# A transformer decoder layer in fp32 on one core: ring order of the cross attention, and row halves for the retention scores

## The reference

```python
# retention, H = 16 heads of HD = 16 channels
ret  = einsum('bhid,bhjd->bhij', q, k) * D            # D: decay mask, causal
ret  = ret / clip(abs(ret.sum(-1)), 1, None)
g    = einsum('bhij,bhjd->bhid', ret, v)
g    = (g - g.mean(-1)) / sqrt(g.var(-1) + 1e-5)      # per head
x    = x + (silu(xn @ Wg + bg) * (g * gn_w + gn_b)) @ Wo + bo
# cross attention, 16 heads, 64 channels after the products of weights
scores = einsum('bhsr,bhlr->bhsl', q_r, k_r)          # 1600 x 1444 for each row of the batch
ctx_c  = softmax(scores) @ kv_r                       # 1444 x 64
x      = x + (ctx_c -> w_kc_kv -> Wo)
# feed-forward with ternary weights
x      = x + bitlinear(sigmoid(x1) * x2, w3)
```

## Time and profile before

| what | us |
|---|---|
| median of 3 runs | 2492.05 |
| the profiled execution's own time | 2489.71 |
| its span | 2487.9 |
| TensorE busy, of the span | 2297.7 (92%) |
| GpSimd busy | 1841.3 (74%) |
| VectorE busy | 1689.2 (68%) |
| ScalarE busy | 1189.3 (48%) |

### The profile page before, as it was taken

The page is one execution under the profiler, slowest core; times in us unless marked ns, Lnnn a source line. Parts: engine busy times, 40 slices in busy tenths (PEclk is TensorE's granted clock), DMA queues, the critical chain, the costliest instruction groups (busy, mean ns, idle before and its releaser), DMA issues. The chain is left out here.

```text
span 2487.9 us, 47277 instructions
## 1 busy us (share of the span) xinstructions
PE 2297.7 (92%) x15380; PEld 1443.5 (58%) x15380; DVE 1689.2 (68%) x2816; ACT 1189.3 (48%) x1925; POOL 1841.3 (74%) x827
## 2 busy tenths in 40 slices
PE   7899857999995999999999999999999999998398
PEld 4454536777772555555555555555555555554388
DVE  5888847888875666666666666666666666660575
ACT  3232312223222665665665665665666666663143
POOL 2444444998883799899899899899898998998111
PEclk9999978999996999999999999999999999999699
DMA  4000015666664424333333333333333343230111
GB/s 136 14 20 20 19 30 158 186 188 172 185 178 115 97 62 90 89 66 85 89 70 84 86 74 86 80 78 86 76 83 83 74 88 83 69 73 13 40 46 40
DMA packets 229954, 212.21 MB, mean 85 GB/s; under 512 B 115542, under 2 KB 204842, under 8 KB 229760
## 3 DMA queue, kind: packets, MB, share of 16 engines
q1 hardware_dynamic: 229888, 211.37, 34.4%
HBM read 128.17 MB, written 59.48 MB: 75 GB/s over the span
## 5 line engine op out<-in xcount | busy, mean ns | idle before, releaser
L1680 POOL TENSOR_TENSOR x_acc<-x_acc,x_prob 120x1600 f32<-120x1600 f32 (+1 forms) x320 | 1154.3, 3607 | 34.0 <-ACT x_prob L1701 11.1
L1701 ACT ACTIVATE x_prob<-x_scores 120x800 f32<-120x800 f32 (+1 forms) x768 | 601.8, 837 | 19.0 <-PE x_scores L1877 11.2
L1897 PE MATMUL x_context<-x_prob,x_kv 120*64 120x400 f32 (+1 forms) x3072 | 600.6, 512 | 0.0
L1796 DVE TENSOR_REDUCE x_mx<-x_ring 115x2 f32<-115x1024 f32 (+1 forms) x341 | 418.2, 1226 | 47.8 <-PE x_ring L1944 29.7
L1805 DVE TENSOR_REDUCE x_mx<-x_ring 115x1 f32<-115x420 f32 (+2 forms) x320 | 199.7, 624 | 225.3 <-PE x_ring L1951 225.3
L1897 PEld LDWEIGHTS x_context<-x_prob,x_kv 120*64 120x64 f32 (+1 forms) x3072 | 186.2, 136 | 261.3 <-issue 261.3
L1721 ACT COPY x_half<-x_ring 115x420 f32<-115x420 f32 (+2 forms) x320 | 171.6, 536 | 329.1 <-PE x_ring L1951 329.1
L1877 PE MATMUL x_scores<-x_qh,x_dh 64*120 64x400 f32 (+1 forms) x1536 | 274.0, 351 | 1.0 <-DMA x_dl<-x_dl 0.3
L1877 PE MATMUL x_scores<-x_ql,x_dh 64*120 64x400 f32 (+1 forms) x1536 | 267.1, 342 | 0.0
L1877 PE MATMUL x_scores<-x_qh,x_dl 64*120 64x400 f32 (+1 forms) x1536 | 266.6, 341 | 0.0
L1809 DVE TENSOR_REDUCE x_mx<-x_half 115x1 f32<-115x420 f32 (+2 forms) x320 | 198.4, 620 | 14.9 <-ACT x_half L1721 13.1
(11 more groups left out here) (179 smaller groups left out, 3682.6 us busy)
## 6 DMA issues: line engine op xcount, KB each, us to landing
x_rden<-scratch_rden SPq DMA_DIRECT2D x68, 200.0 KB, 3.5
scratch_qh<-q_qsh SPq DMA_DIRECT2D x64, 200.0 KB, 3.8
scratch_ql<-q_qsl SPq DMA_DIRECT2D x64, 200.0 KB, 3.8
x_qm<-scratch_qh SPq DMA_DIRECT2D x64, 200.0 KB, 4.2
x_qh<-scratch_qh SPq DMA_DIRECT2D x64, 200.0 KB, 3.4
x_ql<-scratch_ql SPq DMA_DIRECT2D x64, 200.0 KB, 3.9
scratch_kr<-q_krot SPq DMA_DIRECT2D x32, 363.0 KB
x_kr<-scratch_kr SPq DMA_DIRECT2D x32, 363.0 KB
```

What stands on the lines that cost most here:

```text
L1680: pool.tensor_tensor(acc[0:rows, parity], first, prob[0:rows, c % PR], ALU.add).then_inc(acc_done.sem, 1)
L1701: act.activation(prob[0:rows, c % PR, u * HALF:(u + 1) * HALF].rearrange("p (j s) -> p j s", j=2), psc[0:rows, u, :, 0:BANK], ACT.Exp).the ...
L1796: dve.tensor_reduce(best[0:block_rows(r), :, r, i], src[0:block_rows(r), :, 0:b - a], AX.X, ALU.max).then_inc(read_sem(u), 1)
L1897: mm = pe.matmul(pav[DC * s:DC * s + DC, j, 0:BANK], kv[0:rows, parity, c], prob[0:rows, c % PR, cols], start=c == 0, stop=c == LC - 1)
```

## The change

In the cross attention the order of the units changes. Denominators and turn 2 go from chunk 4, behind the context product, to chunk 2, ahead of it; the first wide maximum is made in chunk 0; the last of the maxima of block 6 becomes two halves in chunk 11, where the wide one was. At the end turn 0 stands ahead of the output product. The waits that named the last wide maximum now name the last half or the ready maxima. In the retention each score product works on 64 partitions (4 heads), two of them on different halves of the array one after the other, and `qm` has 4 masked copies instead of 8. The mean is no longer made by itself; the subtraction takes the sum and the factor in one instruction.

```diff
-        headmask = sb("headmask", [P, 8])
+        headmask = sb("headmask", [P, 4])
-        qm = sb("qm", [P, EC, 8, GT])
+        qm = sb("qm", [P, EC, 4, GT])
@@ spread_lower (ScalarE), spread_upper (VectorE)
-                for h in range(8):
+                for h in range(4):
@@ centre
-                dve.tensor_scalar(mean[:], s1[:], 1.0 / HD, None, ALU.mult).then_inc(gn_mean.sem, 1)
-                dve.wait_ge(gn_mean.sem, gn_mean.at(k, 1))
-                dve.tensor_tensor(cent[:], att[:], wide(mean), ALU.subtract).then_inc(gn_centred.sem, 1)
+                dve.scalar_tensor_tensor(cent[:], wide(s1), -1.0 / HD, att[:], ALU.mult,
+                                         ALU.add).then_inc(gn_centred.sem, 1)
@@ scores (TensorE)
-            def scores(k, b, j):
-                c = j // 2
-                pe.wait_ge(sc_masked.sem, sc_masked.at(k, 4 * b + j - 1))
-                pe.matmul(sc[0:S, j % 2, 0:GT], kT[:, c, b * S:(b + 1) * S],
-                          qm[:, c, 4 * (j % 2):4 * (j % 2) + 4, b * S:(b + 1) * S],
-                          start=True, stop=True).then_inc(sc_filled.sem, 1)
+            def scores(k, b, c):
+                for t in range(2):
+                    part = slice(P // 2 * t, P // 2 * (t + 1))
+                    pe.wait_ge(sc_masked.sem, sc_masked.at(k, 4 * b + 2 * c + t - 1))
+                    pe.matmul(sc[0:S, t, 0:GT], kT[part, c, b * S:(b + 1) * S], qm[part, c, :, b * S:(b + 1) * S],
+                              start=True, stop=True).then_inc(sc_filled.sem, 1)
@@ slot (TensorE)
-                    for j in range(4):
-                        scores(k, b, j)
-                        if j == 0 and b >= 2:
+                    for c in range(EC):
+                        scores(k, b, c)
+                        if c == 0 and b >= 2:
                             turn_attn(k, b - 2)
                         if b >= 1:
-                            attend(k, parity, b - 1, j)
+                            for q in range(2 * c, 2 * c + 2):
+                                attend(k, parity, b - 1, q)
@@ phase_cross_attention
-        wide = iter([("max", r, 0) for r in range(0, MB, 2)] + [("max", r, 2) for r in range(MB)])
-        narrow = iter([(r, 1) for r in range(MB)] + [(r, 0) for r in range(1, MB, 2)])
+        wide = iter([("max", r, 0) for r in range(0, MB, 2)] + [("max", r, 2) for r in range(MB - 1)])
+        narrow = iter([(r, 1) for r in range(MB)] + [(r, 0) for r in range(1, MB, 2)] + [(MB - 1, 2)])
...
-            if c not in (0, 5):
+            if c > 0:
                 r, i = next(narrow)
                 own += [("half", r, i, 0), ("half", r, i, 1)]
             own += [("scores", 0), ("scores", 1)]
-            if c > 0:
+            if c == 2:
+                own += [("den", 0), ("den", 1), ("turn", 2)]
+            elif c < LC - 1:
                 own.append(next(wide))
             own.append(("context",))
-            own += {4: [("den", 0), ("den", 1), ("turn", 2)],
-                    LC - 1: [("mT",), ("out",), ("turn", 0), ("turn", 1)]}.get(c, [])
+            if c == LC - 1:
+                own += [("mT",), ("turn", 0), ("out",), ("turn", 1)]
@@ load_qm (SP)
-                    wait_read(sp, n - 3, last_max)
+                    sp.wait_ge(max_ready.sem, max_ready.at(n - 3, 1))
@@ slot (VectorE), the negated maxima
-                            wait_read(dve, n, last_max)
+                            wait(dve, half_read.sem, half_read.at(n, len(copied)))
@@ make (TensorE)
+                if u == first_max and is_at(n, -1):
+                    for i in range(2):
+                        wait_read(pe, n - 1, ("turn", i))
```

More of the change, by code:

```diff
@@ L166, in phase_retention @@
         s1 = sb("s1", [S, GB * H])
-        mean = sb("mean", [S, GB * H])
         cent = sb("cent", [S, GB * H, HD])
@@ L216, in phase_retention @@
         gn_sum = sig("gn_sum", 1)
-        gn_mean = sig("gn_mean", 1)
         gn_centred = sig("gn_centred", 1)
@@ L744, in layout_retention @@
         "rel": np.maximum(rel, 0).astype(np.float32), "causal": (rel >= 0).astype(np.float32),
-        "headmask": np.where(p[:, None] // HD == np.arange(8)[None, :], HD ** -0.5, 0).astype(np.float32),
+        "headmask": np.where(p[:, None] // HD % 4 == np.arange(4)[None, :], HD ** -0.5, 0).astype(np.float32),
         "ident": np.eye(P, dtype=np.float32),
```

## The result

The change made the kernel faster, by less than half of what I forecast: 2474.12 us median of four runs (2472.66 to 2474.59) against 2491.35 of the kernel before on the same chip, ratio 0.9933 with a 95% interval of 0.992 to 0.9945. That is 17.2 us won, where 39.7 were forecast; it lies just outside the range of 2436 to 2474. The profiled execution took 2474.34 us with a span of 2472.6.

What follows compares the result with a forecast made beforehand. TensorE's sequence, with GpSimd's chain close behind, was taken to bound the cross attention, VectorE and GpSimd the retention. Savings of 20.2 + 19.5 = 39.7 us from 2489.7 gave 2450.0, as a median 2452, range 2436 to 2474.

Steps and rivals of the forecast that it cites:

- cross attention: Cross attention slots: three TensorE stops removed, one new stop added; 0.65 saved a slot over 31 slots, 20.2 us.
- (c): Retention: mean fused into the subtraction, which takes over the wait for GpSimd; 0.1 a group, 0.6 us in all.
- (a): Retention: four spreads of 0.34 less on VectorE, 1.36 a group, on the path in all eight groups; 10.9 us.
- (b): Retention: score products as pairs on row halves, 1.0 a pair; saves 8.0 us, bounds 1 and 15.
- turn 1 starts 0.65 ahead of t=0, so it is read at about 1.4, inside the score products: no stop: Cross attention, chunk 0: VectorE finishes reading turn 1 early enough that the new wide maximum, 0.4 long, needn't wait.
- my 45.65: Cross attention: slot length by TensorE alone, from 46.3 less 0.45, 0.35 and 0.1, plus 0.25 for a new stop.
- rival 5: Whole kernel: something in the start or end takes back most of the gain, about 2490 us; chance 0.04.
- The new stop in chunk 2: Cross attention, chunk 2: turn 2 waits for ScalarE, busy with exponentials, to read den; 0.25 lost a slot.
- where the first products come late: Retention, groups 1 to 6, ahead of the variances: 0.84 won where first products are late, taken as 0.45 a group.
- the 3.8: Retention, group 7, which no power holds up: score pairs shorten it from 18.8 to 15, saving 3.8 us.
- number 2: Cross attention gains nothing: ScalarE's chunk 2 reads, GpSimd's moved idle time and mT's wait cancel it; 2472 us, chance 0.17.

Runs made afterwards that it cites:

- Moving the maximum: Changed kernel with no wide maximum in chunk 0 and one in chunk 11 instead: 2454.51 us, ratio 0.9852.
- zero-half keys: Changed kernel with keys written into two tiles, each with the other half of its rows zero, so score products run on all 128 rows: 2470.4 us, ratio 0.9908.
- the run with the first products made twice: Changed kernel with each score product of the first batch element in the retention's first group made twice: 2476.83 us, ratio 0.9946.
- the kernel with the filled wait: Changed kernel with four products of constants on TensorE ahead of each retention group's first score products: 2476.68 us, ratio 0.9945.

## Why the prediction was wrong

**The sum, part by part.** A chain of measured medians from before to after (before 2491.2, cross attention 2488.6, with the fused subtraction 2485.0, with four spreads 2468.6, with pairs 2474.1) puts sizes on the terms:

| term | forecast | measured |
|---|---|---|
| cross attention | 20.2 | 2.5 |
| (c) mean | 0.6 | 3.6 |
| (a) spreads | 10.9 | 16.4 |
| (b) score pairs | 8.0 | -5.5 |
| sum | 39.7 | 17.0 |

These are differences of medians, each uncertain by some 2 to 4 us by the intervals given. By the start of the cross attention in the profiled executions the last three are 2.4, 17.2 and -4.6. The order matters for the last two: with eight spreads the pairs cost 14.6 (2499.65 against 2485.03, which has eight spreads on ScalarE too). The terms are not independent, and a sum of separate prices can't hold that.

**Cross attention: the step that failed** is "turn 1 starts 0.65 ahead of t=0, so it is read at about 1.4, inside the score products: no stop". I took VectorE's 2.02 from turn 2, ahead of which nothing stands. Ahead of turn 1 stands the output addition on the same engine, 0.42 long, and it can't start before the output product has ended. VectorE was through 2.21 after the turn's start, 0.19 later for the addition. Two smaller things came to it: turn 1, without its stop, started 0.51 ahead of t=0 and not 0.65, and from the end of the read to the maximum 0.24 passed, where the earlier trace rows have 0.13. So the turn was read at 1.7 and the maximum started at 1.94 instead of 1.56. This 0.38 is what separates my 45.65 from 46.03, against 45.96 measured. I had priced that same addition where it stopped turn 1 (0.35), removed the stop, and not asked who waits for VectorE next. Moving the maximum showed that this stop was the loss; that the addition makes half of it is read from the rows, no run took it away. The periods fell to 45.43, below my forecast, because the multiplication's wait of 0.19 went with it.

The second miss here is the start. I named a loss at "the start or end" as rival 5 but gave the 31 periods all the same price. The first period grew by 3.4 and the stretch ahead of it by 1.6. Most of the 3.4 goes with the clock and not with the order. In the eleven kernels with a maximum in chunk 0 (the changed one among them) the first period was 45.96 to 49.08, and it followed the time at the low clock inside it: 45.96 with 8.2 us, 46.03 with 8.5, 47.49 with 13.6, 49.08 with 16.3. With like low times (7.6 to 8.3) the order before took 45.04 and 45.35, and without the maximum in chunk 0 it was 44.91 with 8.9. So some 0.9 is the new maximum's price there. What kept the clock down longer, no run settled. The stretch ahead took 40.5 to 40.6 in the three kernels with the order before and 41.7 to 43.3 in the fifteen with a new one, with or without a maximum in chunk 0. That is the order's doing, but which unit costs it was not tested.

**What held in the cross attention.** Both chains end within 0.2 of each other, the seven sums take 25.8, the output product waits for the multiplication by 0.19, turn 1 has no stop, and mT's bank costs nothing. The new stop in chunk 2 was 0.08 and not 0.25: after its exponentials ScalarE read both banks in 1.08 as a pair. What the forecast could have asked and did not is whether the denominators belong in chunk 2 at all: left in chunk 4 they give 45.78.

**Retention: the step that failed** is (b). The products' price was near: I took 1.0 for a pair, and at the full clock one was 0.92 long, as long as the one product on all rows. The Trainium skill (TensorE: Matmul & The Clock Gate, Part 3: Packing small matmuls) has products on different row groups run at the same time; by that rule, the trace agrees: the first pair's two products started within 0.01 us of each other. But the pair's price was not what counted. I had booked 0.45 in each of groups 1 to 6 "where the first products come late". With four spreads the first product was there in time. VectorE in group 3, from the addition ahead of the masks to the end of the variances, with pairs and then with zero-half keys:

```profile
183.55 0.42 DVE L530 TENSOR_TENSOR a_x<-a_po,a_x 100x256 f32<-100x256 f32 x1
...
190.19 0.17 DVE L420 TENSOR_SCALAR a_veps<-a_mv 100x4 f32<-100x4 f32 x1
```

```profile
178.69 0.42 DVE L540 TENSOR_TENSOR a_x<-a_po,a_x 100x256 f32<-100x256 f32 x1
...
185.34 0.17 DVE L430 TENSOR_SCALAR a_veps<-a_mv 100x4 f32<-100x4 f32 x1
```

Both take 6.8, which I had forecast for pairs alone, and the groups' intervals at the full clock were the same, 37.4 to 37.9. So that part of (b) was nothing.

And my bounds, "1 and 15", left out a loss, and no reason excluded one: the price assumed the clock of the earlier trace rows. With pairs, most falls of the clock lasted 10 to 24 us, where they lasted 3.4 to 10 with all rows. In group 7 it was low either way, and the 3.8 there never came: from the last root to the start of the cross attention it took 489.1 on average in the six kernels with the changed retention and 489.6 in the three with four spreads and all rows.

That the pairs prolong the falls is shown by the kernel with zero-half keys, which differs from the changed one in the score products and two copies a group on ScalarE. Whether it is the 64 rows themselves, or that a pair is done sooner, so that TensorE has the stops of 0.70 and 0.19 and less to do, is not shown. The run with the first products made twice, back at 2.4 GHz after 3.4 us on row halves, speaks for the second.

(a) was mis-sized upward: 16.4 on all rows. The intervals of groups 2 to 7 shrank by 1.82 (39.38 to 37.56 on average between the kernels with eight and four spreads on all rows), 1.36 of it the instructions; the remainder goes with the shorter wait ahead of the scores, after which the clock did not fall in groups 2 to 6 of the kernel with four spreads. With eight, the intervals without a fall were 38.86 and 39.06, those with one 39.59 to 39.77. (c) "it is the wait that lasts, and it moves to the fused subtraction" was right for that instruction (2.55), and yet the mean's end brought 2.8 to 3.6, and the wait ahead of group 1's scores was 0.23 shorter without it (3.60 with the fused subtraction alone against 3.83 in the kernel before, 2.27 in the changed kernel against 2.50 with the mean kept). How much of that is the clock I can't separate.

Of the rivals, number 2 (the cross attention gains nothing, 2472) came nearest, but it was near by luck: it rested on ScalarE's reads in chunk 2, which cost 0.08, and left the retention its full 19.5.

**What stays open.** What in a pair keeps the clock down is not shown, as said above. What starts a fall among busy pairs at 34 us, as in the kernel with the filled wait, no run settled. Nor can a single execution's spells be forecast: the same retention code had a low time of 39 to 57 us.

## What to carry to other kernels

When a stop is removed, follow the engine that caused it to its next customer: the work it does late is still late there, and new work put in front of that customer pays for it. Price the first periods of a loop by themselves, and look at the granted clock there before an edit gets the blame. And products packed on parts of the array's rows, cheaper by their own row, can go with a lower clock for everything behind them; where they can be filled to all rows with zeros at no cost, compare both before choosing.

## What the runs showed of the hardware

- After a fall to 1.2 GHz with the same wait ahead of it (2.35 us), score products on 128 rows had the granted clock back at 2.4 GHz in 3.4 us, pairs on 64 rows after 14 to 20 us (five executions of six with the same retention code; in the sixth it did not fall there), although TensorE had no stop over 0.70 and was busy 5.8 to 6.0 us of each 6 from 34 us on. I had not expected the two to differ. The pairs had stops of 0.70 and 0.19 that the 128-row products had not, so the rows alone are not shown to be the cause.
- With products on halves of the rows the clock even fell among them, at 34.8 us, without a stop over 0.70 us ahead of it.
- At 2.4 GHz a pair of float32 products on the two row halves was 0.92 us long, one product on all rows 0.92: two for the price of one. The first pair of group 0 in the changed kernel shows it, and the next pairs, at 1.2 GHz and with a wait for their banks, were 2.13 long:

```profile
30.52 0.92 PE L644 MATMUL a_sc<-a_qm,a_kT 64*100 64x400 f32 x4 [2.35 <-DVE a_qm L487]
32.13 2.13 PE L644 MATMUL a_sc<-a_qm,a_kT 64*100 64x400 f32 x4 [0.70 <-DVE a_ret L456]
```

- The feed-forward varied from 171.2 to 174.1 us with the same code. When the clock rose at its start doesn't explain it: the latest rises, 33.8 and 33.9 us after its first memset, belong to executions of 171.4. In eleven executions the clock fell once more for 3.4 us, some 160 us in, and these took 171.6 to 174.1; the seven without that fall took 171.2 to 171.7.
- In the cross attention's first period a us at 1.2 GHz cost about 0.4 us (my estimate from 45.96 with 8.2 us at the low level and 49.08 with 16.3).
